# A GRU scan with a ternary feed-forward network: the quantisation on VectorE alone, in units of 1024 weights

## The reference

```python
# GRU over 32 time steps, D = 256; xs = x by time step
gi = x_t @ W_ih + b_ih ; gh = h @ W_hh + b_hh
r = sigmoid(i_r + h_r); z = sigmoid(i_z + h_z); n = tanh(i_n + r * h_n)
h_new = (1.0 - z) * n + z * h

# ternary_quant of a weight matrix, in groups of 64 weights, all in bfloat16
w = w_fp32.astype(bfloat16); w_g = w.reshape(-1, 64)
scale = clip(mean(abs(w_g)), 1e-08, None)
q = clip(round(w_g / scale), -1, 1)
w_hat = q * scale
w_q = w + stop_gradient(w_hat - w)

# feed-forward network on every state, H = 1024
gate, up = split(states @ ternary_quant(w_gate_up).T)
hn = rms_norm(silu(gate) * up)
out = x + hn @ ternary_quant(w_proj).T
```

## Time and profile before

| | us |
|---|---|
| median of three runs (377.42 to 377.64) | 377.59 |
| span of the profiled execution, first to last instruction | 376.7 |
| TensorE matmul busy | 350.5 (93%) |
| TensorE weight loads busy | 300.8 (80%) |
| VectorE busy | 258.6 (69%) |
| ScalarE busy | 221.4 (59%) |
| GpSimd busy | 199.3 (53%) |

### The profile page before, as it was taken

The page is one execution under the profiler, slowest core; times in us unless marked ns, Lnnn a source line. Parts: engine busy times, 40 slices in busy tenths (PEclk is TensorE's granted clock), DMA queues, the critical chain, the costliest instruction groups (busy, mean ns, idle before and its releaser), DMA issues.

```text
span 376.7 us, 5881 instructions
## 1 busy us (share of the span) xinstructions
PE 350.5 (93%) x1959; PEld 300.8 (80%) x1962; DVE 258.6 (69%) x484; ACT 221.4 (59%) x434; POOL 199.3 (53%) x165
## 2 busy tenths in 40 slices
PE   6957787788999999999999999999999999999995
PEld 3745566567888889888988888888988898888885
DVE  3499999997586566856585558656685658556644
ACT  5755576554746655666745574665566674547650
POOL 1067765585555536444625555553644472557882
PEclk9998888999999999999999999999999999999998
DMA  7980000370001000100010000100010001000101
GB/s 241 375 359 2 2 0 0 113 334 1 3 3 54 1 2 0 56 0 0 0 56 0 0 0 3 53 0 0 0 56 0 0 0 58 0 0 2 56 2 56
DMA packets 5394, 17.75 MB, mean 47 GB/s; under 512 B 386, under 2 KB 2050, under 8 KB 4996
## 3 DMA queue, kind: packets, MB, share of 16 engines
q1 hardware_dynamic: 5380, 17.57, 12.1%
HBM read 13.38 MB, written 4.19 MB: 47 GB/s over the span
## 4 chain that ended last, share of the span: by engine, by line
PE 75%; DVE 15%; issue 6%; DMA 1%; ACT 1%; SPq 0%; POOL 0%; DVEq 0%; POOLq 0%
PE ps_out L757 15%; PE ps_gate L718 14%; PE ps_up L718 13%; PE ps_rz L699 3%; PE ps_rz L700 3%; PE ps_rz L703 3%; PE ps_n L675 3%; PE ps_rz L675 3%; PE ps_n L676 3%; PE ps_n L678 3%; PE ps_rz L676 3%; PE ps_rz L678 3%; DVE q_sk L571 2%; DVE wguT L578 2%; PE ps_hT L711 2%
## 5 line engine op out<-in xcount | busy, mean ns | idle before, releaser
L311 POOL TENSOR_TENSOR hid_lo<-work,hid_hi 128x512 fp32r<-128x512 f32 x63 | 83.9, 1333 | 123.0 <-ACT hid_hi L378 123.0
L318 POOL TENSOR_TENSOR sq_sum<-sq_sum,work 128x512 f32<-128x512 f32 x54 | 70.8, 1310 | 0.0
L524 DVE TENSOR_TENSOR work<-work,ps_gate 128x512 f32<-128x512 f32 x64 | 43.8, 685 | 38.9 <-ACT work L374 38.1
L718 PE MATMUL ps_up<-grp_hi,wguT 128*128 128x512 f32 x118 | 47.4, 402 | 5.3 <-DVE work L534 5.3
L718 PE MATMUL ps_gate<-grp_hi,wguT 128*128 128x512 f32 x128 | 51.4, 401 | 0.0
L718 PE MATMUL ps_gate<-grp_lo,wguT 128*128 128x512 f32 x128 | 50.8, 397 | 0.0
L378 ACT CAST hid_hi<-work 128x512 fp32r<-128x512 f32 x63 | 38.8, 616 | 19.2 <-DVE work L534 19.2
L350 ACT ACTIVATE rz<-ps_rz 128x512 f32<-128x512 f32 x32 | 19.1, 596 | 50.8 <-PE ps_rz L703 50.8
L498 DVE TENSOR_TENSOR r_hn<-rz,ps_n 128x256 f32<-128x256 f32 x32 | 13.4, 419 | 48.7 <-PE ps_n L678 48.7
L534 DVE TENSOR_TENSOR work<-work,ps_up 128x512 f32<-128x512 f32 x59 | 40.5, 687 | 8.7 <-PE ps_up L718 7.2
L718 PE MATMUL ps_up<-grp_lo,wguT 128*128 128x512 f32 x118 | 46.4, 393 | 0.0
(11 more groups left out here) (115 smaller groups left out, 772.1 us busy)
## 6 DMA issues: line engine op xcount, KB each, us to landing
x_all<-in_x_dram SPq DMA_DIRECT2D x1, 4096.0 KB, 12.2
out_dram<-o_st SPq DMA_DIRECT2D x7, 512.0 KB, 2.7
xT_all<-in_x_dram SPq DMA_DIRECT2D x1, 3072.0 KB, 19.5
x_all<-in_L_ffn_w_gate_up_dram SPq DMA_DIRECT2D x4, 512.0 KB, 9.2
x_all<-in_L_ffn_w_proj_dram SPq DMA_DIRECT2D x1, 1024.0 KB, 12.7
work<-in_L_cond_W_ih_dram SPq DMA_DIRECT2D x2, 384.0 KB, 4.2
work<-in_L_cond_W_hh_dram SPq DMA_DIRECT2D x2, 384.0 KB, 5.9
xT_all<-in_x_dram SPq DMA_DIRECT2D x1, 768.0 KB, 8.4
```

What stands on the lines that cost most here:

```text
L311: nc.gpsimd.tensor_tensor(hid_lo[:, j % RING], hid[:, j % 2], f32(hid_hi[:, j % RING]), ALU.subtract).then_inc(hid_lo_ok, 1)
L318: nc.gpsimd.tensor_tensor(sq_sum[:], sq_sum[:], hid_sq[:, j % 2], ALU.add).then_inc(sq_added, 1)
L524: nc.vector.tensor_tensor(gsg[:, j % 2], sg[:, j % 2], ps_gate[:, j % 2], ALU.mult).then_inc(gsg_ok, 1)
L718: mm = pe.matmul(bank, w, part[:, k].rearrange("p s b -> p (s b)"), start=(k == 0 and i == 0), stop=(k == KD - 1 and i == 1))
```

## The change

There are six units of 1024 weights per partition in the place of twelve of 512: four for the rows of gate and up (both halves of the contraction together) and two for the down projection. Unit u is worked on in step u, all of it in that step. GpSimd's two operations per unit go to VectorE. The chain per unit on VectorE is now `q_half` and `q_scale` (two scalar operations on `q_mean`), `q_keep` = q_half < q_abs, `q_hat` = keep times scale, `q_diff` = q_hat - q_abs, `q_mag` = q_abs + q_diff, all bfloat16, and `signed` = q_mag times sign, written in the matmul's type. `q_keep` was a three-operand operation (scalar_tensor_tensor) and is a two-operand one. On ScalarE `q_mean` of the unit now follows the tanh directly, ahead of `seed_n`, and `q_abs` and `q_sign` of the next unit come at the step's end. In the recurrence `omz` is gone: `zm_n` = (z - 1) n is one operation (scalar_tensor_tensor), and the state is `zh` - `zm_n`.

The core of the diff:

```diff
-                nc.vector.tensor_scalar(omz[:], rz[:, D:2 * D], -1.0, 1.0, ALU.mult, ALU.add)
...
-                nc.vector.tensor_tensor(omz_n[:], omz[:], n_act[:], ALU.mult).then_inc(omz_n_ok, 1)
-                dve.wait_ge(omz_n_ok, t + 1)
-                nc.vector.tensor_tensor(h_nat[:, s % 2, :], omz_n[:], zh[:], ALU.add).then_inc(h_ok, 1)
+                nc.vector.scalar_tensor_tensor(out=zm_n[:], in0=rz[:, D:2 * D], scalar=1.0, in1=n_act[:],
+                                               op0=ALU.subtract, op1=ALU.mult).then_inc(zm_n_ok, 1)
+                dve.wait_ge(zm_n_ok, t + 1)
+                nc.vector.tensor_tensor(h_nat[:, s % 2, :], zh[:], zm_n[:], ALU.subtract).then_inc(h_ok, 1)
...
-        units = [("gu", k, r) for r in (0, HT) for k in range(KD)]
-        units += [("gu", k, r) for r in (4, HT + 4) for k in range(KD)]
-        units += [("pj", 0, j) for j in range(0, HT, 2)]
+        row_tiles = (0, HT, 4, HT + 4)
+        units = [("gu", r) for r in row_tiles] + [("pj", j) for j in (0, 4)]
...
-                nc.gpsimd.tensor_tensor(q_diff[:, b], q_scale[:, b], q_abs[:, u % 4],
-                                        ALU.subtract).then_inc(q_diff_ok, 1)
-                pool.wait_ge(q_diff_ok, u + 1)
-                nc.gpsimd.tensor_tensor(q_mag[:, b], q_abs[:, u % 4], q_diff[:, b],
-                                        ALU.add).then_inc(q_mag_ok, 1)
...
+            def scales(u):
                 dve.wait_ge(q_mean_ok, u + 1)
...
+                nc.vector.tensor_scalar(q_half[:], q_mean[:], 1e-8, 0.5, ALU.max, ALU.mult)
+                nc.vector.tensor_scalar(q_scale[:], q_mean[:], 1e-8, None, ALU.max).then_inc(q_half_ok, 1)
...
             def ternary(u):
...
+                dve.wait_ge(q_half_ok, u + 1)
+                nc.vector.tensor_tensor(q_keep[:], q_half[:], q_abs[:, b], ALU.is_lt).then_inc(q_keep_ok, 1)
                 dve.wait_ge(q_keep_ok, u + 1)
+                nc.vector.tensor_tensor(q_hat[:], q_keep[:], q_scale[:], ALU.mult).then_inc(q_hat_ok, 1)
+
+            def straight_through(u):
+                b = u % 2
+                dve.wait_ge(q_hat_ok, u + 1)
+                nc.vector.tensor_tensor(q_diff, q_hat[:], q_abs[:, b], ALU.subtract).then_inc(q_diff_ok, 1)
+                dve.wait_ge(q_diff_ok, u + 1)
+                nc.vector.tensor_tensor(q_mag, q_abs[:, b], q_diff, ALU.add).then_inc(q_mag_ok, 1)
...
+                nc.vector.tensor_tensor(unit_part(u, wguT, wpT), q_mag, q_sign[:, u % 2],
+                                        ALU.mult).then_inc(q_w_ok, 1)
```

More of the change, by code:

```diff
@@ L102, in gru_ffn @@
         n_act = sb("n_act", [P, D])
-        omz = sb("omz", [P, D])
         zh = sb("zh", [P, D])
-        omz_n = sb("omz_n", [P, D])
+        zm_n = sb("zm_n", [P, D])
         h_nat = sb("h_nat", [P, 2, D])
@@ L115, in gru_ffn @@
         wpT = sb("wpT", [P, HT, D], F32R)
[L116 to L121, removed]
+        q_abs = sb("q_abs", [P, 2, 2, 512], BF16)
+        q_sign = sb("q_sign", [P, 2, 2, 512], BF16)
+        q_mean, q_scale, q_half, q_keep, q_hat = (
+            sb(n, [P, 2, 512], BF16) for n in ("q_mean", "q_scale", "q_half", "q_keep", "q_hat"))
         q_ones = sb("q_ones", [P, P], BF16)
@@ L461, in iteration @@
                         hidden_parts(g - 1, 2 * s - 1)
-                    if not ffn:
-                        for u in summed(g, s):
-                            q_means(u)
                     if ffn:
@@ L602, in iteration @@
                         hidden(g - 1, 2 * s - 1)
-                    early = ffn and s == 1
-                    if early:
-                        for u in finished(g, s):
-                            signed(u)
                     candidate(t, s)
@@ L610, in iteration @@
                         input_lo(t + 2, s % 2)
-                    if not early:
-                        for u in finished(g, s)[:1]:
-                            signed(u)
-                    for u in summed(g, s)[:1]:
-                        scale_and_mask(u)
+                    for u in unit_of(g, s):
+                        scales(u)
                     if ffn:
@@ L632, in iteration @@
                         hidden(g - 1, 0)
-                    if not early:
-                        for u in finished(g, s)[1:]:
-                            signed(u)
-                    for u in summed(g, s)[1:]:
-                        scale_and_mask(u)
-                    for u in summed(g, s):
+                    for u in unit_of(g, s):
                         ternary(u)
+                        straight_through(u)
+                        signed(u)
                     if carry and s == 0:
@@ L792, in q_group_sums @@
                 pe.wait_ge(q_abs_ok, u + 1)
-                if u >= 2:
-                    pe.wait_ge(q_mean_ok, u - 1)
-                pe.matmul(q_sum_bank(u), q_ones[:], q_abs[:, u % 4],
-                          start=True, stop=True).then_inc(q_sum, 1)
+                if u:
+                    pe.wait_ge(q_mean_ok, u)
+                for a in range(2):
+                    mm = pe.matmul(q_sums[:, a], q_ones[:], q_abs[:, u % 2, a, :], start=True, stop=True)
+                mm.then_inc(q_sum, 1)
             def ffn_item(g, item):
```

120 lines of the change are left out of this document (38 added, 82 removed).

## The result

The changed kernel takes 368.18 us (median of 4 runs, 365.51 to 368.48); the kernel before, run beside it, 377.5 (377.17 to 377.64). The ratio of the two is 0.9729, 95% interval 0.9696 to 0.9763: 2.7% faster. The profiled execution has a span of 366.7 us where it was 376.7, and is itself the run of 368.48 us.

What follows compares the result with a forecast made beforehand. VectorE was taken to bound the kernel up to some 93 us, TensorE after; step gains of 10.4 less 0.8 for the clock took 9.6 off the 376.7 us span, giving 367.1, with 0.9 for the median 368.0; range 365.0 to 371.8.

Steps and rivals of the forecast that it cites:

- VectorE per unit: Operation lengths per unit of 1024: q_half and q_scale 0.43 us each, four bf16 operations 0.69 each, signed 1.22.
- step 0: First quantisation step: 8.0 us in the place of 9.22, step 1 starting at 24.6, gain 1.2 us.
- steps 1 and 2: Quantisation steps, from r_hn to the next: 7.57 us each in the place of 9.91, gain 4.7 us together.
- Step 3: Quantisation step with its copy: 8.05 us where it was 10.40, gain 2.3 us.
- Step 4: Quantisation step where hid_lo stops VectorE once: 11.6 us where it was 13.03, gain 1.4 us.
- Step 5: Last quantisation step, gated waiting 1.1 us and GpSimd stopping VectorE twice: 13.6 us where it was 12.69, loss 0.9.
- Step 6: Step without quantisation: TensorE's 1.59 us wait before an up product goes, gain 1.6 us.
- The clock: TensorE stands 2.5 us in step 5; a clock fall would cost up to 1.7 us, half taken, 0.8.
- TensorE would stand only 0.4 us in steps 1 to 3: TensorE's stand before the transposes of steps 1 to 3, 2.5 to 3.1 us before, would be some 0.4 us.
- the clock of 1.00 from 26 to 60 us: Sign of being right: TensorE's granted clock at 1.00 from 26 to 60 us; before, 0.83 from 26 to 36.
- a stand of more than 2 us: Sign of being wrong: TensorE still standing more than 2 us before the transposes.

Runs made afterwards that it cites:

- changed_again: The changed kernel once more, unaltered, to see its spread; 368.25 us, ratio 0.9743 to the kernel before.
- no_fold: The changed kernel with the 1-z operation put back in the recurrence; 366.92 us, ratio 0.9721 to the kernel before.
- side_writes: The changed kernel with two GpSimd memsets of scratch data beside VectorE's unit in each of steps 0 to 2; 367.32 us, ratio 0.9725.
- fill: The changed kernel with eight throwaway matmuls of 128 columns on TensorE ahead of an up product in step 6; 366.76 us, ratio 0.9726.
- mean_early: The changed kernel with q_mean moved ahead of the tanh on ScalarE from step 1 on; 367.82 us, ratio 0.9746.
- split_last: The changed kernel with q_diff, q_mag and signed of unit 5 moved from step 5 to the end of step 6; 364.5 us, ratio 0.9654.

## Why the prediction was right

The forecast was 368.0 us, the result 368.18. The mechanism held: VectorE paces steps 0 to 5, GpSimd beside it is what stretched its operations, and the part after 93 us didn't change. Two terms were off and made up for each other, and one statement on TensorE's waits was wrong.

- *VectorE per unit*: 0.42, 0.69 and 1.22 us measured, for 0.43, 0.69 and 1.22. The comparison is packed. The 58 cycles in the table of the Trainium skill (VectorE: DVE Perf Modes, section on the TRN2 errata), by which the sum would have been 3 us lower, are too few for all of them (0.42 us for 256 float32 elements, by the table 0.33). The same section says so below its table and gives about 150 cycles as the measured fixed term, which these rows agree with; the prediction quoted only the table.
- *Steps*: 8.0 forecast for step 0, 7.86 measured; 7.57 for steps 1 and 2, 7.55 and 7.56. Step 3: 8.05, measured 8.66 and, in changed_again, 8.42; `zm_n` started 0.42 us after the tanh's end there (in step 5 it was 0.03) and no row says why, so that stays open. The 0.24 us between the two are the clock's: in the changed kernel it is 0.77 from 41 to 42 us and 0.50 from 42 to 44, the transpose at 41.65 takes 0.69 us for changed_again's 0.44, and the low part is later by as much. Step 4: 11.6, measured 11.15 (the stop by `hid_lo` cost 1.0, not 1.2, and the rest of the chain was shorter). Step 5: 13.6, measured 13.28, with the forecast wait of 1.1 us (1.06) and two stops of 1.0 each. `r_hn` of steps 1 to 6 came at 23.9, 31.4, 39.0, 47.6, 58.8 and 72.1 for the 24.6 to 73.0 of the prediction, 0.2 to 0.9 us earlier. 0.6 of that is the start of step 0, which varies from profile to profile and is no success of the prediction.
- *Step 6*: the wait before the up product of tile 5 is gone, as forecast, and TensorE has no gap from 76 to 330 us.
- *The clock*: the stand was forecast at 2.5 us and is 2.47. Half of 1.7 us was taken for it; the whole 1.5 fell due in both profiles of the changed kernel, and nothing in those of no_fold and side_writes with the same stand. A half was neither outcome.
- *Luck*: without the clock the steps were forecast to gain 10.4 us, and gained 10.9 to 11.1 (76.63 against 65.72 in side_writes and 65.53 in fill, which have no fall); steps 4 and 5 gave 0.8 more than forecast, step 0 0.1 and step 6 0.3, step 3 0.4 to 0.6 less. The clock took 1.5 for the 0.8 put down. So 9.4 us remain for the 9.6 of the sum. That the median is right to 0.2 us is these two misses cancelling, on top of runs that themselves lie 3 us apart (365.51 to 368.48).
- *What was wrong* is the sentence that TensorE would stand only 0.4 us in steps 1 to 3, and with it the clock of 1.00 from 26 to 60 us. It stands 1.96, 0.59 and 2.12 us before the transposes of steps 1 to 3, and the clock is at 0.83 from 26 to 36 us as before, and from 36 to 46. The prediction had named a stand of more than 2 us as a sign of being wrong, and the 2.12 is one:

```profile
26.16 0.44 PE L627 MATMUL ps_hT<-ident,h_nat 128*128 128x128 f32 x2 [1.96 <-DVE h_nat L435]
...
33.71 0.44 PE L627 MATMUL ps_hT<-ident,h_nat 128*128 128x128 f32 x2 [0.59 <-DVE h_nat L435]
...
41.65 0.69 PE L627 MATMUL ps_hT<-ident,h_nat 128*128 128x128 f32 x2 [2.12 <-DVE h_nat L435]
```

The prediction gives no working for the 0.4 us; it is what is left of the 2.81 us of step 2 before when the step's 2.34 are taken off. But TensorE's work ahead of that stand had run in part at the lower clock (0.50 from 29 to 32 us). At the full clock the same work is shorter and the stand longer. mean_early shows it, whose clock is 1.00 through step 1:

```profile
26.88 0.44 PE L631 MATMUL ps_hT<-ident,h_nat 128*128 128x128 f32 x2 [1.97 <-DVE h_nat L439]
...
34.43 0.44 PE L631 MATMUL ps_hT<-ident,h_nat 128*128 128x128 f32 x2 [1.97 <-DVE h_nat L439]
```

In the changed kernel the clock is low from 28 to 31 us, and the next stand is 0.59. So a short stand and a full clock, both of which the prediction had, don't go together here. It cost next to nothing: VectorE paces these steps, steps 1 and 2 are 7.55 us with either clock, and step 3 lost 0.24. The rows of before also left open what stands between 1.64 and 2.5 us do to the clock: here it fell after one of 1.96 us, and in split_last after one of 1.75, but not after the first 1.97 of mean_early, though after its second, nor after 2.38 in side_writes.

## What to carry to other kernels

An operation moved to GpSimd is not simply taken off VectorE where both read SBUF at the same time: here 24 operations went from GpSimd to VectorE, and the seven steps became 7.5 us faster. Find the step in which the two pacing engines change places, and count gains only up to it. Then clear the pacing engine just enough in the last steps before it (three operations moved by one step gave 3.7 us more). Before an engine's wait is removed by starting a third engine earlier, look at what that engine then runs beside.

## What the runs showed of the hardware

- A GpSimd addition lengthened a VectorE operation with two SBUF inputs by 0.7 us (1.41 for 0.69), a GpSimd memset by nothing. A scalar operation on bf16 beside GpSimd's reading operations took 1.52 us for 0.42, in mean_early, and `gated`, which reads PSUM, its 0.69 us beside `sq_sum` in the changed kernel.
- The same stand of TensorE, 2.47 or 2.48 us, was followed by the lower clock in four profiles of six. Of shorter stands, 1.96 and 1.75 us were followed by it too, one of 1.97 and one of 2.38 us were not, and once the clock fell with no stand before it. The fall cost 1.5 us where TensorE set the pace, nothing in steps 1 and 2 and 0.24 us in step 3, where VectorE did.
- A three-operand operation on bf16 took 1.22 us for 1024 elements, a two-operand one 0.69.
